# A quantised grouped convolution on 32 images: three quarters of the last image stored in two transfers each

## What is computed

```python
def block(v):                                   # v = group_norm(x), 32 groups
    xg = v.reshape(B, 4, 128, H, W)[:, [1, 2, 3, 0]]
    xa = round(clip((xg - lA) / (uA - lA), 0, 1) * 15) / 15
    wq = (round(clip((weight - lW) / (uW - lW), 0, 1) * 15) / 15 - 0.5) * 2
    y = einsum('bgihw,goi->bgohw', xa, wq.reshape(4, 128, 128)).reshape(B, C, H, W)
    inv = gamma / sqrt(running_var + 1e-5)
    return relu(y * inv + (beta - running_mean * inv)) + v
out = x + block(group_norm(x))
```

## Time and profile before

| | us |
|---|---|
| median of 3 runs | 259.68 |
| lowest and highest | 259.65, 260.01 |
| the profiled execution's own time | 259.98 |
| its span, first to last instruction | 258.3 |
| last instruction of DVE that computes ends | 248.7 |
| SP's last wait for a store is over | 257.8 |

### The profile page before, as it was taken

The page is one execution under the profiler, slowest core; times in us unless marked ns, Lnnn a source line. Parts: engine busy times, 40 slices in busy tenths (PEclk is TensorE's granted clock), DMA queues, the critical chain, the costliest instruction groups (busy, mean ns, idle before and its releaser), DMA issues.

```text
span 258.3 us, 4030 instructions
## 1 busy us (share of the span) xinstructions
PE 190.6 (74%) x999; PEld 109.4 (42%) x999; DVE 229.5 (89%) x363; ACT 215.4 (83%) x394; POOL 213.5 (83%) x340
## 2 busy tenths in 40 slices
PE   1142995987788898668598787979966878998930
PEld 0132654553444555344364444454633535464410
DVE  2898698799999989999979999998999998999950
ACT  4338898889999998999978999989899997989600
POOL 6126869998999999899999999999989999989500
PEclk9999997699979779999859997986999995999995
DMA  6999999999999999999999999999999999999994
GB/s 216 394 413 411 409 407 410 415 415 419 416 417 415 413 416 417 413 417 418 412 417 417 416 418 417 412 415 416 415 417 417 416 413 408 402 399 393 381 385 158
DMA packets 34520, 103.28 MB, mean 400 GB/s; under 512 B 1202, under 2 KB 1730, under 8 KB 34498
## 3 DMA queue, kind: packets, MB, share of 16 engines
q1 hardware_dynamic: 18624, 54.86, 53.5%
q10 hardware_dynamic: 15874, 48.18, 46.8%
HBM read 51.65 MB, written 51.38 MB: 399 GB/s over the span
## 4 chain that ended last, share of the span: by engine, by line
POOL 35%; DVE 21%; PE 20%; issue 17%; DMA 2%; DVEq 1%; SPq 0%; POOLq 0%; ACT 0%
POOL images L411 17%; PE prod L594 14%; DVE images L482 9%; DVE stats L456 7%; POOL levels L421 6%; PE var_ps L584 5%; POOL dev L372 3%; DVE codes L471 3%; DMA images<-in_x 2%; POOL norm L399 1%; POOL dev L375 1%; POOL newt L395 1%; POOL scaled L401 1%; POOL newt L396 1%; POOL newt L397 1%
## 5 line engine op out<-in xcount | busy, mean ns | idle before, releaser
L594 PE MATMUL prod<-codes,w_t 128*128 128x392 bf16 x768 | 155.6, 357 | 18.1 <-DVE images L482 11.9
L482 DVE SCALAR_TENSOR_TENSOR images<-prod,floor,images 128x784 f32<-128x784 f32 x128 | 127.9, 1020 | 11.0 <-PE prod L594 10.8
L411 POOL TENSOR_SCALAR images<-images,coef 128x784 f32<-128x784 f32 x120 | 128.6, 1083 | 0.0
L594 PEld LDWEIGHTS prod<-codes,w_t 128*128 128x128 bf16 x768 | 76.4, 107 | 88.8 <-issue 43.1
L267 ACT ACTIVATE levels<-images,coef 128x784 int16<-128x784 f32 x95 | 91.5, 1028 | 0.4 <-POOL coef L403 0.4
L456 DVE BATCH_NORM_STATS2 stats<-images 128x6 f32<-128x392 f32 x136 | 68.9, 551 | 5.2 <-DMA images<-in_x 5.2
L240 ACT ACTIVATE unused<-images,sums 128x784 bf16<-128x784 f32 x60 | 56.1, 938 | 0.1
L234 ACT ACTIVATE unused<-images 128x784 bf16<-128x784 f32 x60 | 50.7, 846 | 6.2 <-DMA images<-in_x 5.1
L471 DVE TENSOR_SCALAR codes<-levels 128x3136 bf16<-128x3136 int16 x32 | 34.2, 1070 | 1.0 <-POOL levels L421 1.0
L421 POOL TENSOR_SCALAR levels<-images,coef 128x784 int16<-128x784 f32 x33 | 32.9, 997 | 0.1
L584 PE MATMUL var_ps<-dev,avg 128*128 128x8 f32 x128 | 21.9, 299 | 14.5 <-POOL dev L379 14.5
(11 more groups left out here) (66 smaller groups left out, 80.1 us busy)
## 6 DMA issues: line engine op xcount, KB each, us to landing
images<-in_x SPq DMA_DIRECT2D x30, 1568.0 KB, 13.2
out<-images ACTq DMA_DIRECT2D x30, 1568.0 KB, 17.5
images<-in_x SPq DMA_DIRECT2D x8, 392.0 KB, 6.6
out<-images SPq DMA_DIRECT2D x1, 1568.0 KB, 8.6
out<-images SPq DMA_DIRECT2D x4, 392.0 KB, 6.5
w_raw<-in_weight SPq DMA_DIRECT2D x1, 256.0 KB, 6.4
rows<-in_channel_params ACTq DMA_DIRECT2D x1, 8.0 KB, 2.4
limit_row<-in_limits ACTq DMA_DIRECT2D x1, 0.0 KB
```

What stands on the lines that cost most here:

```text
L411: nc.gpsimd.tensor_scalar(here, here, coef[:, u % 2, 0, 1, G * j + o:G * j + o + 1], coef[:, u % 2, 1, 1, G * j + o:G * j + o + 1], ALU.mu ...
L482: nc.vector.scalar_tensor_tensor(out=two, in0=prod[:, k % SETS, :, 0:HALF], scalar=floor[:, o:o + 1], in1=two, op0=ALU.max, op1=ALU.add).t ...
L594: done = nc.tensor.matmul(prod[:, k % SETS, h, 0:HALF], w_t[:, part, output_group(g)], codes[:, n % 2, g, h * HALF:(h + 1) * HALF], start= ...
```

## The change

The table `LAST_ROWS = (4, 8, 12, 0)` gives for each quarter of the last image a number of rows that are stored by a transfer of their own. The first three quarters are stored as 124 and 4, 120 and 8, 116 and 12 rows; the fourth still as 128. The small transfers follow the large ones on SP without a wait, and count up a semaphore of their own, for which SP waits once more at the end. No other engine's program changes.

```diff
+LAST_ROWS = (4, 8, 12, 0)
...
+        stored_rest = sem("stored_rest")
...
             for g in range(G):
                 o = output_group(g)
                 sync.wait_ge(final, G * (B - 1) + g + 1)
-                sync.dma_start(out_v[B - 1][:, o], images[:, (B - 1) % RING, o]).then_inc(stored[(B - 1) % RING], DMA)
+                j, cut = (B - 1) % RING, P - LAST_ROWS[g]
+                sync.dma_start(out_v[B - 1][0:cut, o], images[0:cut, j, o]).then_inc(stored[j], DMA)
+                if cut < P:
+                    sync.dma_start(out_v[B - 1][cut:P, o], images[cut:P, j, o]).then_inc(stored_rest, DMA)
             for j in range(RING):
                 stores = len(range(j, B, RING)) + (G - 1 if j == (B - 1) % RING else 0)
                 sync.wait_ge(stored[j], DMA * stores)
+            sync.wait_ge(stored_rest, DMA * sum(rest > 0 for rest in LAST_ROWS))
```

## The result

| | before | changed |
|---|---|---|
| median of 6 runs, us | 259.78 | 268.56 |
| lowest and highest | 259.65, 261.27 | 267.22, 270.42 |
| profiled execution, its span | 259.98, 258.3 | 270.42, 268.7 |

The ratio is 1.0334, with a 95% interval of 1.0302 to 1.0366: 8.7 us slower (7.8 to 9.5). The profiled execution of the changed kernel is the slowest of its six, 1.9 us above their median.

A forecast was written before the change was run, and what follows sets the result against it. The prediction took the 16 DMA engines emptying their store queues as the bound at the end. Four engines with 47 more rows at 0.125 us, weighed over five cases, gave 259.68 + 4.2 = 263.9 us, range 262.0 to 269.4.

The forecast's parts named there:

- What bounds the end: After DVE's last quarter at 248.7 us, the end is set by how fast 16 DMA engines empty their queues.
- late engine: At the end of the stores, one DMA engine works until 257.1 us, 3.2 us or 25 rows behind ten others.
- queues never run dry: On the four engines with more rows, image 30 lasts until about 249.9 us; the 124 rows are issued at 245.9.
- Equal shares on up to 16 engines: Each store uses the most engines, up to 16, that divide its rows evenly: 124 rows on 4, 120 on 15.
- The same four engines for 124 and 116: Both large pieces fall on the same four engines: 79 rows instead of 32, 47 more, 5.9 us.
- How late the latest of the four is: End of the four engines with more rows: five cases from +2.7 to +5.9 us, middle +4.2.
- the case of +5.9: The latest engine, ending at 257.1 us, is among the four with 47 more rows; chance 1 in 4.
- Every row at 0.125 us: In the final stores a row costs an engine 0.125 us, whether 16 engines work or one alone.
- second rival: Four engines with 31 rows each meet in SBUF, half of 60 rows at half rate: +3.75 us, 267.7; chance 0.20.
- Three more issues: SP's added issues take 1.1 to 3.8 us in all, hidden behind the four engines' rows, costing nothing.
- The late engine relieved: Rows dealt over 16 engines as they come, the last loses 20: 258.4 to 258.8 us; chance 0.18 with related cases.
- Theory P: Experiment forecast for halves by row: two engines share one SBUF reading place, rows of 0.25 us, +4 us over gated before.

The follow-up runs named there:

- gated kernel: Kernel before, with SP waiting for DVE's last finished quarter ahead of the stores of images 30 and 31; 1.0094 of the kernel before, +2.4 us.
- halves by column: Kernel before with that same wait, each last-image quarter stored as two transfers of all 128 rows with half the columns; 1.0081 of the kernel before, +2.1 us.
- all engines started together: Changed kernel with SP waiting for DVE's last quarter ahead of the stores of images 30 and 31; 1.0500 of the kernel before, +13.0 us.
- kernel with equal shares: Kernel before with the last image's first three quarters each split into 112 and 16 rows; 1.0040 of the kernel before, +1.0 us.

## Why the prediction was right and wrong

The range held the time (268.56 in 262.0 to 269.4), and the sign was right. The forecast of +4.2 us was a little less than half of the 8.7 that came. That the range held is in part luck: it was stretched to 269.4 for a case with a chance of 0.20, and in that case the slow rows were to be on four engines only.

- **What bounds the end.** Right. The late engine's backlog is visible by itself in the gated kernel at 246 to 249 us. That the queues never run dry was read too broadly: before, the share was already 0.67 at 245 us, and in the changed kernel it was 0.68 at 247, so some engines had nothing to do before image 30 came.
- **Equal shares on up to 16 engines.** Right, by the packet count of every changed kernel, and by price from 2.1 us (92 rows on four) to 13.4 us (127 on one). The counts agree with the Trainium skill, "DMA: Bandwidth & Descriptors", section "Why a DMA increments its semaphore by 16 and not by 1", in all these numbers of rows. The same four engines for 124 and 116: right, by the share of about 0.25 from 254 to 260 us with the small ones last.
- **How late the latest of the four is.** This term of the sum was in all likelihood mis-sized. I took the middle of five cases, +4.2; the prices (2.9 of 3.0 us for 124 and 4 rows, 5.8 of 5.9 for all seven transfers with the small ones last) fit the case of +5.9, the late engine itself among the four, to which I gave one chance in four. Slow rows are in some of these prices, so it is not proved. An engine alone with 127 rows costs 13.4 of 15.0 us (interval 12.1 to 14.7), so that one is not the latest itself.
- **Every row at 0.125 us.** This is the step that failed: the sum priced all 47 added rows at 0.125 us and put slower rows at nothing. In the profile of the change the busy engines moved 16 GB/s each from 251 to 263 us, not 25. What I had named as the sign of my second rival came, a stretch at a share of about 0.25 with 44 to 82 GB/s (254 to 257 us), in place of 100 GB/s for four to six microseconds. That rival had +3.75, but as a matter of four engines with long blocks among themselves. 124 rows alone showed none of it, while nine engines at 122 rows and all of them at 120 rows were slow. What the slow rows have in common is a quarter cut by rows; the three kernels whose stores all span the 128 partitions (before, gated before, halves by column) fall below 22 GB/s an engine in no window with a share near 1. That several engines then read the same part of SBUF is the best guess, not shown. The sum that stands now is 5.9 for the shares and 2.8 for slow rows, 8.7 us, and 4.6 with all engines started together; the second part is what is left over, not measured by itself, and if the late engine is not among the four it is larger.
- **Three more issues.** Hidden, as said, but not small: SP's last issue ended 9.7 us after the first began, not 5.2. An issue of 31 or 29 rows an engine was taken to be short; the one of 116 rows took 3.1 us. In the kernel with equal shares three more issues and slow rows show as 1.0 us together.
- **The late engine relieved.** Out. The rows are not dealt over 16 engines as they come, the engine that 120 rows spare is not the late one (+0.5 us, not -1), and no kernel here was faster than before.

**What stays open.** Why rows are slow. Theory P, if it holds, gives half the rate; some rows in the changed kernel's windows are slower than that, 11 GB/s for an engine at 254 us. The last rows of each quarter, 4, 8 and 12 of them, lie next to each other, so four and more engines may meet there; this was not tried apart. Nor was a cut by rows whose pieces leave the writes as they are. Nor is it known why one engine is late. And the times of the changed kernel spread more (267.2 to 270.4, again 265.9 to 271.6) than those of before. The profiles have image 30's store at 242.6 to 248.0 us. In the kernel before, an engine that is late anyway may hide that moment; in the changed one it may set how far apart the engines are, and so whether they meet. That is argued from one profile a kernel, and not uniform: with 16-row pieces there are slow rows with the store issued at 243.1, with 124 and 4 none at 242.8.

## What to carry to other kernels

Leave a store over all 128 partitions whole at the end, where nothing hides it. Where rows have to be cut, choose their number so that 16 divides it: 124 rows took 4 engines and 127 took one, at 0.125 us a row or more, and the end waits for the engine with the most. That is not enough by itself, as 112 and 16 rows still cost 1.0 us; a cut by columns over all partitions was 1.4 us cheaper than one by rows. And when all DMA engines look busy, divide the rate by the share: 25 GB/s for each was the healthy figure here, and less meant that the rows themselves were slow.

## What the runs showed of the hardware

- A transfer whose rows fall on few engines holds up the issue of the next ones: 4.2 us for an issue of one row behind 127 rows on one engine, and later, from 253 to 255 us, 15 engines idle while three quarters waited behind it.
- All 16 engines were busy at 238, 220 and 270 GB/s while pieces cut by rows were stored, where they move 401 with whole quarters. The DMA share alone would not have told.
- An engine of 16 was 3.2 us late at the end of 250 us of even work. Such an engine hides delay in the others: image 30's store went out at 249.1 us in the gated profile against 245.0 before, 4.1 later, and the gate cost 2.4 us.
